# The causal mask of a diagonal chunk: one full-height product instead of two half-height ones

## The reference

```python
scores = jnp.einsum('bhqd,bhkd->bhqk', q, k)
causal = j <= i
scores = jnp.where(causal[None, None], scores, NEG)
...
w = jax.nn.softmax(scores, axis=-1)
```

## Time and profile before

| | us |
|---|---|
| median of 3 runs | 1968.99 |
| lowest and highest | 1961.76, 1969.76 |
| the profiled execution | 1967.3 |
| its span, first to last instruction | 1965.5 |
| TensorE busy in the span | 1680.7 (86%) |
| VectorE busy | 1428.1 (73%) |
| ScalarE busy | 1127.5 (57%) |
| GpSimd busy | 695.3 (35%) |
| mean granted clock of TensorE | 0.889 of full |

### The profile page before, as it was taken

How to read it: one execution, slowest core, us unless ns; L and a number is a source line. 1 busy time by engine, 2 the same in 40 slices (tenths; PEclk the granted TensorE clock), 3 DMA queues, 4 the chain that set the end, 5 groups by cost and what they waited for, 6 DMA issues and landing times.

```text
span 1965.5 us, 36378 instructions
## 1 busy us (share of the span) xinstructions
PE 1680.7 (86%) x12410; PEld 1039.2 (53%) x12410; DVE 1428.1 (73%) x3057; ACT 1127.5 (57%) x1999; POOL 695.3 (35%) x788
## 2 busy tenths in 40 slices
PE   6899999999978799987788999999999777889910
PEld 5545444445556677774334454544446566777710
DVE  5678888888577865885547788888865787558843
ACT  2145767577557677764233558585674676776710
POOL 6000101000257556445660001010012674754466
PEclk9678989899979999998895789898998898999965
DMA  6540120300065656665752204031002555666643
GB/s 233 173 70 2 24 45 13 56 2 2 31 265 165 182 172 199 207 198 184 239 188 50 32 2 64 4 49 18 2 7 101 217 175 166 204 189 201 203 146 118
DMA packets 127906, 225.96 MB, mean 115 GB/s; under 512 B 15364, under 2 KB 91028, under 8 KB 123444
## 3 DMA queue, kind: packets, MB, share of 16 engines
q1 hardware_dynamic: 103152, 156.49, 26.4%
q0 software_dynamic: 24576, 67.14, 12.5%
HBM read 124.20 MB, written 98.84 MB: 113 GB/s over the span
## 4 chain that ended last, share of the span: by engine, by line
PE 57%; DVE 12%; DMA 11%; issue 7%; POOL 7%; ACT 3%; SPq 1%; ACTq 0%; DVEq 0%; POOLq 0%
PE late_banks L1721 14%; PE late_banks L1679 12%; PE exp_banks L1707 8%; PE late_banks L1510 6%; PE exp_banks L1527 6%; POOL ring_t L1086 4%; DMA ring_t<-token_rows,index_t 4%; DMA ring_t<-expert_rows,rows_of_t 3%; DVE inter_t L2020 3%; POOL ring_t L1081 2%; DVE chunk_max_t L2139 2%; DMA expert_rows<-outs_t 2%; PE late_banks L1485 2%; PE late_banks L1685 2%; PE late_banks L1543 2%
## 5 line engine op out<-in xcount | busy, mean ns | idle before, releaser
L1339 ACT ACTIVATE probs_t<-exp_banks 128x1024 f32<-128x1024 f32 (+3 forms) x640 | 539.2, 896 | 294.6 <-PE exp_banks L1707 292.0
L2139 DVE TENSOR_REDUCE chunk_max_t<-late_banks 128x1 f32<-128x512 f32 (+1 forms) x960 | 603.0, 682 | 115.8 <-PE late_banks L1679 89.6
L1177 POOL TENSOR_SCALAR_AFFINE_SELECT probs_t<-probs_t 128x512 f32<-128x512 f32 x128 | 81.2, 635 | 681.5 <-ACT probs_t L1339 681.5
L1721 PE MATMUL late_banks<-probs_t,values_t 128*32 128x512 f32 (+3 forms) x2560 | 320.0, 575 | 1.9 <-POOL probs_t L1177 1.1
L1086 POOL DMA_INDIRECT ring_t<-expert_rows,rows_of_t x256 | 243.7, 952 | 188.9 <-DVE x_sb_t L2038 126.6
L1510 PE MATMUL late_banks<-tokensT_t,fetched_t 128*128 x2048 | 297.5, 290 | 11.5 <-ACT fetched_t L1243 5.1
L1081 POOL DMA_INDIRECT ring_t<-token_rows,index_t x256 | 248.7, 972 | 140.5 <-PE late_banks L1485 83.4
L2020 DVE TENSOR_TENSOR inter_t<-late_banks,silu_t 64x256 f32<-64x256 f32 x512 | 217.5, 425 | 89.1 <-ACT silu_t L1260 78.2
L1510 PEld LDWEIGHTS late_banks<-tokensT_t,fetched_t 128*128 128x128 f32 x2048 | 254.1, 195 | 41.9 <-issue 23.0
L1679 PE MATMUL late_banks<-contextT_t,Qp_t 50*128 50x512 f32 (+7 forms) x640 | 234.4, 515 | 9.6 <-DVE chunk_max_t L2139 2.2
L1527 PE MATMUL exp_banks<-fetched_t,inter_t 64*128 64x128 f32 x2048 | 187.6, 303 | 45.8 <-DVE inter_t L2020 43.7
(11 more groups left out here) (228 smaller groups left out, 1886.4 us busy)
## 6 DMA issues: line engine op xcount, KB each, us to landing
expert_rows<-outs_t SPq DMA_DIRECT2D x256, 256.0 KB
weights_t<-in_experts SPq DMA_DIRECT2D x8, 1728.0 KB, 13.8
Qp_t<-q_rows SPq DMA_DIRECT2D x12, 768.0 KB
weights_t<-in_experts SPq DMA_DIRECT2D x4, 2112.0 KB, 10.4
q_rows<-part_hi_t SPq DMA_DIRECT2D x16, 512.0 KB, 3.9
k_rows<-part_hi_t SPq DMA_DIRECT2D x16, 512.0 KB, 4.5
Kp_t<-k_rows SPq DMA_DIRECT2D x8, 768.0 KB
q_rows<-part_lo_t SPq DMA_DIRECT2D x16, 256.0 KB, 5.1
```

The source lines that it names most:

```text
L1339: act.activation(probs[:, e % NP, 2 * p:2 * p + 2, off:QB], exp_banks[sq % 2][:, :, off:QB], ACT.Exp, scale=D ** -0.5).then_inc(exp_done, 1)
L1721: last = pe.matmul(pv_banks[n % NPV][32 * h:32 * h + 32, off:QB], values[:, j, GH * g + h, :], probs[:, e % NP, h, off:QB], start=(j == 0) ...
L2139: op = dve.tensor_reduce(chunk_max[:, b, p, chunk_row(r), chunk_col(b, r, c)], bank[:, 0:n].rearrange("q (p k) -> q p k", p=len(parts)), A ...
```

## The change

The mask is added by one product on all 128 rows, for the heads of both halves alike. `ident16` and `cut16` become plain copies in bf16 of `ident` and `cut`, made by two casts in place of eight. It adds 128 columns in one go. Nothing else changes: not the score products, not the planner's order or its costs, not the reductions.

```diff
-        ident16 = tile("ident16", [P, 2, P], BF16)
-        cut16 = tile("cut16", [P, 2, P], BF16)
+        ident16 = tile("ident16", [P, P], BF16)
+        cut16 = tile("cut16", [P, P], BF16)
...
-                    for a in range(2):
-                        for to in range(2):
-                            rows, of = slice(to * HALF, (to + 1) * HALF), slice(a * HALF, (a + 1) * HALF)
-                            pool.wait_ge(ident_ready, 2 + 4 * a + 2 * to)
-                            pool.tensor_copy(ident16[rows, a, :], ident[of, :]).then_inc(ident_ready, 1)
-                            pool.wait_ge(ident_ready, 3 + 4 * a + 2 * to)
-                            pool.tensor_copy(cut16[rows, a, :], cut[of, :]).then_inc(ident_ready, 1)
-                    pool.wait_ge(ident_ready, 10)
+                    pool.wait_ge(ident_ready, 2)
+                    pool.tensor_copy(ident16[:, :], ident[:, :]).then_inc(ident_ready, 1)
+                    pool.tensor_copy(cut16[:, :], cut[:, :]).then_inc(ident_ready, 1)
+                    pool.wait_ge(ident_ready, 4)
...
-                pe.wait_ge(ident_ready, 10)
+                pe.wait_ge(ident_ready, 4)
...
                             last = pe.matmul(bank[:, begin:end], Qp[s][rows, p, t * P:(t + 1) * P],
                                              Kp[s][rows, p, c * QB:c * QB + end - begin], start=True, stop=c < b)
                             if c == b:
-
-                                rows = slice(hh * HALF, (hh + 1) * HALF)
-                                for a in range(2):
-                                    last = pe.matmul(bank[:, end - P + a * HALF:end], ident16[rows, a, :],
-                                                     cut16[rows, a, a * HALF:P], start=False, stop=a == 1)
+                                last = pe.matmul(bank[:, end - P:end], ident16[:, :], cut16[:, :], start=False, stop=True)
```

## The result

The changed kernel takes 2207 us (median of 4 runs, 2199 to 2219) against 1966 us of the kernel before, timed alongside: 1.124 times as long, 95% interval 1.120 to 1.127. That is 241 us more. The forecast was 2163 us, 2060 to 2280. Every ratio in this text leaves out the executions that lie over 1.5% above the fastest of their kernel.

A forecast was written before the change was run, and what follows sets the result against it. TensorE was taken to bound attention almost everywhere. The profiled execution's 1967.3 us + 176 for TensorE's added time - 25 swallowed by idle time + 45 for clock falls gave 2163 us, range 2060 to 2280.

The forecast's parts named there:

- A change of height costs a gap of 0.09 us each way, and the weight load stands bare: Around each full-height mask on TensorE: two empty gaps of 0.09 us, product 0.07, unhidden weight load 0.11, together 0.36 us.
- +0.277 us a part: TensorE's added time per diagonal part at full clock: 0.504 us after the change against 0.227 before.
- The ideal pairing: Both halves of TensorE always filled before the change: 0.17 us a part, making the added time +0.337 us.
- The sum for TensorE less what is swallowed, 151 us: Attention's 377 warm and 135 cold parts add 176 us on TensorE, of which idle time takes 25.
- my 25: Added TensorE time hidden by its idle time in each layer's first phases: 25 us, between none and 50.
- the surcharge of the 135 cold parts: Diagonal parts at half clock were charged +0.53 us each, 72 us together, against +0.277 for warm ones.
- I take seven: +45: Seven of 19 further attention phases bring a fall of TensorE's clock, 6 to 7 us each: +45 us.
- Rival 1: TensorE's clock falls in nearly every attention phase: 2258 us, chance 0.13.
- The casts: On GpSimd, eight casts become two, some 2 us less, hidden by the projections: cost and gain zero.
- A barrier without gaps: The full-height mask enters TensorE as soon as both halves are empty: 2013 us, chance 0.08.
- a cover by VectorE: VectorE's ten reductions set each attention phase and hide a third of TensorE's added time: 2059 us, chance 0.06.
- The Trainium skill's spacing: Mask products on TensorE cost columns over 2.4 GHz plus 2.5 ns, whatever the rows: some 15 us gained.

The follow-up runs named there:

- e5_all_full: The changed kernel with the diagonal parts' score products also 128 rows high, scores and softmax not the reference's: 1999 us against 1963 of the kernel before.

## Why the prediction was right

- **What bounds attention.** Right: TensorE, nearly everywhere. 239 of the 243 us between the spans lie in the attention stretches.
- **A change of height costs a gap of 0.09 us each way, and the weight load stands bare.** Right to the last digit that the rows give (0.47 against 0.475 us for 256 columns), and e5_all_full, where mask and score have one height, has 0.01 us in place of 0.16 between their loads.
- **+0.277 us a part.** Somewhat too much: 0.225 in the phase that stayed at full clock. The ideal pairing, my upper bound, was further off still. By e5_all_full the larger part of it, 0.13, is the other half's lost work and not the gaps.
- **The sum for TensorE less what is swallowed, 151 us.** Measured at equal clock: 99 us. The 32 phases of 16 parts at 0.23 us would be 118, so some 19 us are swallowed, near my 25. Of the 52 us between 151 and 99, 34 are the surcharge of the 135 cold parts, which belongs to the clock's side of the account; the rest is the 0.277.
- **The clock, "I take seven: +45".** This is the term that was mis-sized. Half clock in attention went from 206 to 557 us, and it reached into 30 of the 32 phases; that is 140 us by the fit, where I had 45 + 34. Rival 1, the fall in nearly every phase, to which I gave 0.13, had the mechanism as it came out. Its 2258 us was 51 too many: its sum leaves out the 25 us swallowed that every other one takes off, and it stood on the larger price of a part. The forecast value lay 44 us short, since the clock's side was 61 too small and the rest 18 too large; that it came so near owes something to these two having opposite signs. The seven falls were a guess between none and all 19, not worked out from a row.
- **The casts.** GpSimd's two casts last 0.29 us each, the bias addition starts at 30.02 in place of 32.47, and TensorE's first mask at 59.7: no effect, as said.
- **The rivals.** A barrier without gaps (2013 us) and a cover by VectorE (2059 us) are excluded by the 0.16 us of the rows and by VectorE, busy 3.90 of 5.40 us inside a phase. The Trainium skill's spacing in "TensorE: Matmul & The Clock Gate", section "Back-to-back issue gap", by which the change would have gained, is given there for an isolated product; here it fits products of one height (0.05 us for each mask more in the last phases) and not a change of height (0.16 us from a mask's load to the next).

The casts in the changed kernel, on GpSimd's timeline:

```profile
27.49 0.29 POOL L1142 CAST ident_t<-ident_t 128x128 bf16<-128x128 f32 x1
27.73 0.29 POOL L1143 CAST cut_t<-cut_t 128x128 bf16<-128x128 f32 x1
...
30.02 9.06 POOL L1153 TENSOR_TENSOR x_sb_t<-x_sb_t,bias_rows_t 128x4096 f32<-128x4096 f32 x1
```

## What to carry to other kernels

Where products of half the array's height run in pairs, a full-height product among them is no cheaper for being one instead of two: it costs two empty gaps, bares a weight load, and takes the other half's work away (0.225 us a part here at full clock, 0.13 of it for the last). Keep small helpers at the height of their neighbours, or gather them so that the height changes seldom; and when a change puts gaps between products, price the fall of TensorE's clock from stretches of the same trace where it fell, in all the places that become like them, for it can cost more than the gaps.

## What the runs showed that I had not expected

TensorE's clock fell in phases in which the engine is busy in the windows from end to end (5.40 of 5.40 us ahead of the fall shown), and adding useless products to the same order brought it back: 573 us of half clock in attention with two masks a part, 318 with three, 193 and 242 with four, so that four were faster than one. Whether the short gaps or the emptier array makes it fall, no run here separates. And a half-height mask can be nearly free (14 to 19 us for 1024) while the same mask once more is not (57 us).
